# Moving the expert layer's matmul operands to fixed addresses modulo 256 bytes

## The reference

```python
xn = _layernorm(x)
x = x + attention(xn) + ffn(xn)
# attention: 16 heads of 16, scores times a decay mask, no softmax, then a group norm
# ffn: 8 experts, each takes its best 128 tokens of every sequence
scores = jnp.einsum('BTC,CE->BTE', xn, gate_w)
top_p, top_idx = jax.lax.top_k(transpose(softmax(scores)), 128)
h = gelu(jnp.einsum('BElC,ECH->BElH', xin, w1))      # C = 256, H = 1024
y = jnp.einsum('BElH,EHC->BElC', h, w2) * top_p
out = zeros.at[b_idx, top_idx].add(y)
```

## The kernel before

| | stationary | moving |
|---|---|---|
| layer 1 | w1: 0 | xs: 64 |
| layer 2 | g: 64 | w2: 0 |
| projections of the attention stage (`product`, L1383) | w_hi, w_lo: 0 | x_hi, x_lo, a_hi, a_lo: 0 |

## Time and profile before

### The profile page before, as it was taken

One profiled execution on the slowest core, in us unless ns is written; L12 is line 12 of the kernel. 1 busy time (PEld: TensorE's weight loads), 2 busy tenths in 40 slices (PEclk: granted clock), 3 DMA queues, 4 the chain that ended last, 5 costly groups with the idle time before them and its releaser, 6 DMA issues.

```text
span 2307.2 us, 81411 instructions
## 1 busy us (share of the span) xinstructions
PE 2224.3 (96%) x34252; PEld 2060.6 (89%) x34252; DVE 1527.1 (66%) x3103; ACT 1391.4 (60%) x2553; POOL 1281.3 (56%) x2012
## 2 busy tenths in 40 slices
PE   6999999999999987999999999999999999999998
PEld 5777777778777767999999999999999999999998
DVE  2555555566667656997677677676676676676675
ACT  5555565555566544656566666666666666666664
POOL 4444444444554443755566676676676666666553
PEclk9999999999999999999999999999999999999999
DMA  3232222222222221333234234233233333332332
GB/s 121 70 98 88 77 77 76 93 87 85 77 76 84 96 76 58 52 85 46 48 56 81 49 54 83 49 53 83 51 51 83 51 49 85 52 51 45 53 49 35
DMA packets 129368, 157.72 MB, mean 68 GB/s; under 512 B 11008, under 2 KB 118656, under 8 KB 129024
## 3 DMA queue, kind: packets, MB, share of 16 engines
q0 software_dynamic: 49152, 67.14, 18.1%
q1 hardware_dynamic: 79872, 85.54, 11.6%
HBM read 85.53 MB, written 67.11 MB: 66 GB/s over the span
## 4 chain that ended last, share of the span: by engine, by line
PE 54%; DVE 0%; POOL 0%; issue 0%; ACT 0%; DVEq 0%
PE attn L1779 28%; PE scores L1698 17%; PE front L1698 7%; PE front L1688 2%; POOL out L798 0%; DVE rows L211 0%; DVE topi L207 0%; DVE top L202 0%; DVE hidden L1263 0%; DVE xs_lo L1233 0%; ACT res L949 0%; DVE rows L223 0%; PE scores L233 0%; PE scores L232 0%; DVE rows L225 0%
## 5 line engine op out<-in xcount | busy, mean ns | idle before, releaser
L1779 PE MATMUL attn<-w_hi,g_hi 128*128 128x256 f32 x2048 | 577.2, 282 | 0.3 <-ACT y L949 0.3
L1779 PE MATMUL attn<-w_lo,g_hi 128*128 128x256 f32 x2048 | 571.2, 279 | 0.0
L1779 PE MATMUL attn<-w_hi,g_lo 128*128 128x256 f32 x2048 | 571.1, 279 | 0.0
L987 ACT ACTIVATE hidden<-hidden 128x512 f32<-128x512 f32 x384 | 235.3, 629 | 259.6 <-DVE hidden L1263 259.5
L1779 PEld LDWEIGHTS attn<-w_hi,g_hi 128*128 128x128 f32 x2048 | 386.7, 189 | 0.6 <-ACT y L949 0.5
L1779 PEld LDWEIGHTS attn<-w_lo,g_hi 128*128 128x128 f32 x2048 | 386.3, 189 | 0.0
L1779 PEld LDWEIGHTS attn<-w_hi,g_lo 128*128 128x128 f32 x2048 | 384.5, 188 | 0.0
L1698 PE MATMUL scores<-xs_hi,w_hi 128*128 128x256 f32 x1280 | 359.1, 281 | 9.4 <-DVE xs_lo L1233 6.8
L1698 PE MATMUL scores<-xs_hi,w_lo 128*128 128x256 f32 x1280 | 356.5, 279 | 0.0
L1698 PE MATMUL scores<-xs_lo,w_hi 128*128 128x256 f32 x1280 | 356.5, 279 | 0.0
L1263 DVE TENSOR_TENSOR hidden<-front,hidden 128x512 f32<-128x512 f32 x256 | 176.3, 689 | 267.0 <-PE front L1698 256.5
(11 more groups left out here) (182 smaller groups left out, 5149.0 us busy)
## 6 DMA issues: line engine op xcount, KB each, us to landing
x<-in_x SPq DMA_DIRECT2D x32, 512.0 KB, 4.5
w_stage<-in_w SPq DMA_DIRECT2D x16, 1024.0 KB
xn_rows<-xn SPq DMA_DIRECT2D x32, 512.0 KB, 3.0
res<-in_x SPq DMA_DIRECT2D x32, 512.0 KB, 3.9
out<-res SPq DMA_DIRECT2D x32, 512.0 KB, 3.2
xg<-xn_rows,step_idx POOLq DMA_INDIRECT x256
out<-y,scatter_idx POOLq DMA_INDIRECT x128
out<-res,scatter_idx POOLq DMA_INDIRECT x128
```

The costliest lines, as they stand in the source:

```text
L987: act.activation(own(q, p), src, ACT.Gelu).then_inc(g_ready, 1)
L1779: last = pe.matmul(yb[k % 2][:, 0:D], g_[:, m, cols], w, start=start and m == first and i == 0, stop=end, skip_group_check=True)
```

## The change

Only offsets change. `g_hi`, `g_lo` and the buffers placed relative to them (`hidden`, `y`, `x_sums`) move up by 192 bytes, to residue 0. `xs_hi`, `xs_lo` move up by 448 bytes, to residue 192. All parts of w2 move to residue 192, as does the staging buffer `w2_stage`, which also changes places with one half of a low part of w2. w1 stays at residue 0. After the change every stationary operand of both layers is at residue 0 and every moving one at 192. No instruction, wait, order or size changes.

```diff
@@ -384,23 +384,25 @@
 
         SL = GRP * CAP
         HALF = SL // 2
-        G_AT = 87 * KB + 64
-        X_AT = 143 * KB + 64
-        w1h = [at("w1_hi0", [P, 7, QF], F32R, 183 * KB + 512), at("w1_hi1", [P, 7, QF], F32R, 57 * KB)]
-        w1l = [at("w1_lo0", [P, 7, QF], F32R, 197 * KB + 512), at("w1_lo1", [P, 7, QF], F32R, 169 * KB + 512)]
-        s2 = at("w2_stage", [P, FT, D], F32, 211 * KB + 512)
-        w2h = [at("w2_hi0", [P, FT, D], F32R, 79 * KB), at("w2_hi1", [P, FT, D], F32R, 157 * KB + 512)]
+        MOVED = 192
+        G_AT = 87 * KB + 256
+        X_AT = 143 * KB + 256 + MOVED
+        LATE = 183 * KB + 512
+        w1h = [at("w1_hi0", [P, 7, QF], F32R, LATE), at("w1_hi1", [P, 7, QF], F32R, 57 * KB)]
+        w1l = [at("w1_lo0", [P, 7, QF], F32R, LATE + 14 * KB), at("w1_lo1", [P, 7, QF], F32R, LATE - 14 * KB)]
+        s2 = at("w2_stage", [P, FT, D], F32, LATE + 32 * KB + MOVED)
+        w2h = [at("w2_hi0", [P, FT, D], F32R, 79 * KB + MOVED), at("w2_hi1", [P, FT, D], F32R, X_AT + 14 * KB)]
         w2l = [[at(f"w2_lo{i}{j}", [P, FT // 2, D], F32R, o) for j, o in enumerate(os)]
-               for i, os in enumerate(((71 * KB, 75 * KB), (165 * KB + 512, 219 * KB + 512)))]
+               for i, os in enumerate(((71 * KB + MOVED, 75 * KB + MOVED), (X_AT + 22 * KB, LATE + 28 * KB + MOVED)))]
         xg = [at(f"xg{k}", [P, D], F32, (53 + k) * KB) for k in range(GRP)]
         g_hi = at("g_hi", [P, FT, SL], F32R, G_AT)
-        g_lo = at("g_lo", [P, FT, SL], F32R, G_AT + FT * SL * 4)
+        g_lo = at("g_lo", [P, FT, SL], F32R, G_AT + 16 * KB)
         hid = {q: at(f"hidden{q}", [P, 2, 2, HALF], F32, G_AT + o * KB)
                for q, o in (("22", 32), ("21", 36), ("11", 44), ("12", 48))}
         y = [at("y", [P, GRP, D], F32, G_AT + 40 * KB), res]
         xsum = at("x_sums", [P, 4, HALF], F32, G_AT + 52 * KB)
         xs_hi = at("xs_hi", [P, 7, HALF], F32R, X_AT)
-        xs_lo = at("xs_lo", [P, 7, HALF], F32R, X_AT + 7 * HALF * 4)
+        xs_lo = at("xs_lo", [P, 7, HALF], F32R, X_AT + 7 * KB)
 
         xb_ = {p: sbk[:, i, :] for i, p in enumerate("AB")}
         zb = sbk[:, 2:4, :]
```

## The result

The changed kernel took 2279.31, 2285.06, 2286.18 and 2331.02 us, median 2285.62; the kernel before took 2309.76 beside it (2306.33 to 2318.17). The ratio is 0.9885, 95% interval 0.9864 to 0.9906; it leaves the 2331.02 us out as a disturbed run, and the experiments show that this time belongs to the kernel.

The account below looks back on a forecast made before the run. The prediction took TensorE's stream of matmuls in the expert stage as the bound: 2309.1 us, less 26 for all-short steps, less 2 for early steps, gives 2281 us; range 2277 to 2312.

Parts of the forecast that it names:

- Jumps of residue turn the cadence, and without one at the change of layer it is carried on: Expert-stage matmuls: 113.3 or 117.8 ns; residue jumps from layer 1 to 2 turn this; constant residues end that turning.
- Which state?: Expert stage after 1060 us: all short taken, 26.1 us less, because attention matmuls at constant residues become short; chance 0.52.
- rows 5: Layer 2's timeline before the change: at the 192 spacing, 117.7 ns held for all 42 matmuls of a run.
- The rival that the long cadence locks in: Expert stage: a stream long when the early waits end stays slow in all 57 steps; about 2330 us, chance 0.20.
- The rival that the transposes alone turn it: Expert stage: steps alternate between 21.27 and 22.08 us; 2306 us, chance 0.22 for turning at the transposes or otherwise.
- The price of a step: Expert stage after 1060 us: a step falls from 21.725 to 21.27 us if all short, 26.1 us over 57.4 steps.
- The early steps: Some 8 steps before 1060 us, with TensorE's waits for layer 1's operands: between 0 and 3.6 us gained, 2 taken.
- The rule that denies it: TensorE's two independent read ports never wait, so addresses could not matter: time stays at 2309 us, chance 0.06.
- Other engines' buffers: Buffers of VectorE, ScalarE and GpSimd at other residues: costed at nothing, VectorE having 117 us idle in 400.
- The load of w2: Load landing at residue 192: estimated 38 beats for 32, hidden by the 40 us before its first read.
- Another engine as the bound: VectorE's waits for TensorE, 251 us in 57 waits, against a step 0.455 us shorter: nothing binds, no chance given.
- the two runs of a layer that the prediction compares: Runs of each layer in steps near 1505 and 1527 us, at 113.3 and 117.8 ns, said to have the same data.

Follow-up runs that it names:

- const_64_0: Against the kernel before: every stationary operand at residue 64, every moving one at 0, in both layers; 2311.82 us, ratio 0.9991.
- xg192: The changed kernel with the gathered rows, stationary operand of the transposes, at residue 192 in place of 0; 2308.48 us, ratio 0.9986 to the kernel before.
- xg128: The changed kernel with the gathered rows, stationary operand of the transposes, at residue 128 in place of 0; 2285.80 to 2286.64 us, ratio 0.9889 to the kernel before.

## Why the prediction was right, point by point

- *Jumps of residue turn the cadence, and without one at the change of layer it is carried on*: held at the changes of layer. Of the kernels with one pair for both layers none turned there after 1060 us. At the transposes it is no rule: const_64_0 and xg192 turned at them, xg128 kept the short cadence over a jump, and the changed kernel turned at 972.04 us with every stationary operand at 0.
- *Which state?* Here the reasoning failed and the forecast came out by luck. I took short because the attention stream at (0, 0) settles to 113.3 ns by itself. In the expert stage (0, 0) is the worst of the pairs tried, 119.9 ns. What a pair does to 512-column matmuls behind other work did not carry over. The bound that I set against it, rows 5, was the better guide: at a spacing of 192 both cadences hold, and waits, hitches and other matmuls in the stream choose.
- *The rival that the long cadence locks in* was put at 0.20 and 2330 us. The price was right (2331 to 2336) and the chance too small: 4 of 10. Its mechanism fits, but no such execution was profiled. If it holds, the forecast and this rival are both true of the same kernel, in different executions; the mean gain is 5 to 9 us and not 26.
- *The rival that the transposes alone turn it*, 2306 us, is not this kernel, but it is what const_64_0 and xg192 do, at 2311.82 and 2308.48.
- *The price of a step*: 21.27 us forecast, 21.29 measured; 24.4 us over 56 steps, against 26.1 over 57.4.
- *The early steps*: 2 us forecast, none gained. They hang on VectorE's operands, and a faster stream waits more: 11.1 us in the group that had 9.4.
- *The rule that denies it* was rightly set aside. The Trainium skill (SBUF — State Buffer, Who interferes with whom) has TensorE wait on nobody at its two read ports. The runs do not agree with what the prediction drew from it, that addresses could not matter: steps of 21.29 to 22.46 us in kernels that differ in buffer offsets alone.
- *Other engines' buffers* cost nothing that shows: VectorE's `low_of_g` (L1276) takes 684 ns, before 685, ScalarE's GELU (L989) 630, before 629. *The load of w2*, issued at 1247.11 us, is first read at 1286.37, as covered as before.
- *Another engine as the bound*: VectorE's waits for TensorE fall from 251.2 us to 233.9, far from none.
- *Two statements to set right*: by the diff, `xs_hi` and `xs_lo` moved up by 384 bytes (from 143 KB + 64 to 143 KB + 448) and not by 448; the residue of 192 is as told. And the data are not the same in the two runs of a layer that the prediction compares, as each step holds other tokens. That this does not matter is seen in the changed kernel, where all 55 steps after 1060 us take 21.29 us.

## What to carry to other kernels

When a stream of equal matmuls shows two cadences and nothing is waited for, look at the addresses of both operands modulo 256 bytes, and time each pair on the stream itself; a pair that is good in another stage says little. Where a stream can hold two cadences, time many executions and look for two clusters: a median of four, or a ratio of the fastest, hides the part that went the other way. A constant pair does not settle by itself which cadence it holds; to profit every time, something in the loop should lead back to the short one, as the transposes at residue 64 did in two traces here, at 0.01 us a step.

## What the runs showed of the hardware

- At a granted clock of 1.00 (1500 to 1900 us of each trace), 256-column float32r matmuls followed each other in 113.3 to 119.9 ns, in kernels that differ in offsets alone. After 1060 us these were, as (stationary, moving): 113.3 or 117.8 at (0, 192) and at (64, 0), 117.8 at a constant (0, 64), and as means of a step 117.4 at (0, 160), 118.3 at (0, 224), 118.7 at (0, 128), 119.9 at (0, 0). At (0, 192) and at (64, 0) each of the two cadences was kept over changes of layer.
- After 1060 us the eight transposes kept the short cadence (rows at 0 or 128 beside (0, 192); no long stream met them there in a profile), turned it (at 192; at 0 beside (64, 0), from 1121 us on), or ended a long cadence after two steps and then left the short one alone (at 64). Before 1060 us those at 0 beside (0, 192) turned it twice in one trace. I found no rule for which does what; it stays open.
- After a wait of 3.24 us TensorE ran at 118 ns a matmul for 1 us and then for about 3 us at the lower clock level: 213 ns, and a granted clock of 0.61 in this stretch of the changed kernel's table:

```profile
1035.20:1039.60 4.40, 4.40 (x25) 4.40 (x26) 3.41 (x6) 1.97 (x4) 1.47 (x1) 0.61 0.02 4
```
